# One more product of two identities on TensorE at each step of the first four edge passes

## The chip, the cores and the metric

One core of a Trainium2 chip. The time is the device time of one execution, in microseconds (us); of several executions the median is given.

## What is computed

A graph network of four layers over 3125 nodes of 256 features and 50,000 edges. The edges are sorted by destination. Every layer gathers a row per edge by its source, weights it, and sums the rows by destination; then come dense products, the residual and a layer norm.

```python
def _layernorm(x, axis=-1, eps=1e-05):
    m = jnp.mean(x, axis=axis, keepdims=True)
    v = jnp.var(x, axis=axis, keepdims=True)
    return (x - m) / jnp.sqrt(v + eps)

x = _layernorm(x + L0(x, src, dst, edge_weight))   # h=(1+eps)x+segment_sum(w*x[src],dst); relu(h@w1+b1)@w2+b2
x = _layernorm(x + L1(x, W, att, src, dst))        # 4 heads: softmax of leaky_relu(es[src]+ed[dst]) per dst, sum of alpha*z[src]
x = _layernorm(x + L2(x, ...))                     # two such attention layers (4 heads of 64, then 1 of 64), self loops added
x = _layernorm(x + L3(x, ...))                     # query-key attention, layer norm, FFN of 512, layer norm
```

Layer L2 has two passes over the edges, the others one each: five passes, called L0, L1, L2a, L2b and L3 in the code.

## The kernel before

The edges are cut into 416 steps (`STEPS`) of 128 edges, each within one block of 128 destination nodes. A pass runs over all steps. One step:

- GpSimd (POOL, L617) gathers the step's 128 source rows from a table in HBM by an indirect DMA into a slot of a ring (24 slots in L0, 48 in the others). It waits for `step_summed` of the step that had the slot before.
- The rows are scaled by their weight: in L0 by ScalarE (L1826, by the edge's weight), in L1 and L2a by VectorE (L1179), in L2b by VectorE (L1182), in L3 by ScalarE (L1887). This counts `row_scaled` up. In the last two groups of L1 and L2a (`HELPED`) ScalarE and GpSimd do a part of it.
- TensorE (PE) multiplies the step's one-hot matrix `M` (128 edges by 128 nodes of the block) with the rows into one of four PSUM banks (three in L3): L1551 in L0, L1655 in the others. It waits for the scaled rows, and for `sum_added` of the step that had the bank before. It counts `step_summed` up.
- VectorE adds the bank to the block's sums in `ACC` (L980 in L0, L1208 in the others, L1206 at a group's first step) and counts `sum_added` up.

All data is fp32, except where named. L0 also makes the one-hot matrices (VectorE, L966) and stores them to HBM; the later passes load them. Every 12 steps of L0 a small product on PE (L1541) transposes the destinations of 16 steps for VectorE (L905 to L915), which waits for it in the order of its own work.

The later passes work in groups of 16 steps (`GS`). For the softmax, a group's logits are picked (PE, L1607; in L3 `spread`, L1578, a product of 258 columns at each step, dotted with the rows by VectorE, L1084), transposed (L1616), scanned along the edges by VectorE (L1093 to L1164) with small products of PE between (L1623, L1628, L1635), exponentiated by ScalarE (L1850) and turned back (L1640). The sums run 32 steps behind the picks (`SOFAR` is 31). Each engine's order is written out in one loop over steps; on VectorE the addition of a step stands three positions behind the scaling, so that step k's rows are scaled right behind the addition of step k-4, which frees step k's bank.

Between the passes dense stages run (L1692, L1709, L1730). The change touches `sum_edges` (first pass) and `sum_step` in `gat_edges` (the other four), both on PE. `mm` is PE's matmul; `ident` is the 128 by 128 identity in fp32.

```python
for k in range(STEPS):                                                   # L0, PE
    pe.wait_ge(onehot_made.sem, onehot_made.at("L0", k + 1))
    pe.wait_ge(row_scaled.sem, row_scaled.at("L0", k + 1))
    if k >= 4:
        pe.wait_ge(sum_added.sem, sum_added.at("L0", k - 3))
    mm(PS[k % 4][:, 0:D], M[:, k % (4 * G), :], rows[:, k % RING["L0"], 0:D], start=True, stop=True)
```

## Time and profile before

| what | value |
|---|---|
| median of three runs | 3743.68 us (3743.38 to 3746.13) |
| the profiled execution | 3751.99 us |
| its span, first to last instruction | 3750.2 us |
| PE / PEld / DVE / ACT / POOL busy | 65% / 44% / 54% / 21% / 59% |
| mean granted clock of TensorE | 0.708 |
| DMA | 474.15 MB, 126 GB/s |

PE is TensorE's matmuls, PEld its weight loads, DVE VectorE, ACT ScalarE, POOL GpSimd. PEclk is the granted clock, as a share of full speed (2.4 GHz); it has two levels, 1 and 0.5. A fp32 product stands in the trace as two matmul instructions. Where the profile names "remote" or "another core or an unknown queue" as what ended a wait, it found no instruction that had ended shortly before the semaphore changed; this kernel has one core.

The first pass runs from 66 to 668 us, the others from 806, 1511, 2206 and 2985 us.

### The profile page before, as it was taken

The page shows a single profiled execution, that of the slowest core. Times are in us where ns is not written, and L with a number is a line of the kernel's source. Part 1 is how long each engine was busy: PE and PEld are TensorE (multiplying, and loading weights), DVE is VectorE, ACT ScalarE, POOL GpSimd, SP SyncE. Part 2 cuts the span into 40 slices and gives each one's busy share as a digit, 9 for nine tenths or more (in the row PEclk, how much of TensorE's full clock was granted, in tenths as well). Part 3 has the DMA queues.
Part 4 walks back from the last instruction along what each step waited for, and adds up shares of the span by engine and source line. Part 5 has one row for each costly group of instructions (what it writes and reads, how often), then busy time and mean ns, then how long its engine had stood idle before and what let it go on. Part 6 is the DMA issues. An engine that isn't in the chain of part 4 may idle for free.

```text
span 3750.2 us, 44316 instructions
## 1 busy us (share of the span) xinstructions
PE 2421.6 (65%) x9759; PEld 1656.7 (44%) x9759; DVE 2018.7 (54%) x7443; ACT 797.5 (21%) x2126; POOL 2225.6 (59%) x2434
## 2 busy tenths in 40 slices
PE   3564555936776774577677724444466688888887
PEld 1333333714444443344444514444453455555566
DVE  3554444626666674466666713333353366666677
ACT  1444445400000013000000300000002234443432
POOL 3666666466666646676666366666634366666535
PEclk8767666956666676566766755555555799999999
DMA  5665565145555543455555223333322255554411
GB/s 150 172 171 171 167 172 170 51 135 153 158 159 156 157 117 104 139 161 154 154 160 156 55 66 90 91 91 90 89 66 78 76 153 150 150 151 146 143 43 42
DMA packets 293515, 474.15 MB, mean 126 GB/s; under 512 B 63703, under 2 KB 166252, under 8 KB 293263
## 3 DMA queue, kind: packets, MB, share of 16 engines
q0 software_dynamic: 93184, 233.79, 23.9%
q1 hardware_dynamic: 200079, 237.52, 21.1%
q8 instruction: 95, 1.56, 0.2%
q14 instruction: 157, 1.29, 0.1%
HBM read 416.18 MB, written 54.91 MB: 126 GB/s over the span
## 4 chain that ended last, share of the span: by engine, by line
PE 45%; issue 21%; another core or an unknown queue 12%; DVE 11%; POOL 4%; ACT 2%; DMA 2%; DVEq 1%; SPq 0%; ACTq 0%; POOLq 0%
PE PS L1655 22%; PE PS L1578 5%; POOL work L617 4%; PE PS L1709 4%; PE PS L1551 4%; DVE ACC L1208 3%; PE PS L1730 2%; DVE work L1179 1%; PE PS L1692 1%; DMA work<-in_x,srcK 1%; PE PS L1635 1%; PE PS L1607 1%; PE PS L1764 1%; PE PS L1765 1%
## 5 line engine op out<-in xcount | busy, mean ns | idle before, releaser
L617 POOL DMA_INDIRECT work<-t_z,srcK x1248 | 1228.2, 984 | 635.4 <-issue 305.9
L1655 PE MATMUL PS<-work,M 128*128 128x260 f32 (+3 forms) x3328 | 1300.1, 511 | 469.2 <-issue 216.1
L1655 PEld LDWEIGHTS PS<-work,M 128*128 128x128 f32 x3328 | 750.6, 269 | 703.3 <-issue 494.6
L1208 DVE TENSOR_TENSOR ACC<-ACC,PS 128x260 f32 (+3 forms) x1614 | 589.3, 365 | 238.6 <-PE PS L1655 108.9
L617 POOL DMA_INDIRECT work<-t_x,srcK x416 | 395.7, 951 | 280.3 <-PE PS L1655 153.3
L617 POOL DMA_INDIRECT work<-in_x,srcK x416 | 397.3, 955 | 252.9 <-issue 116.0
L1551 PE MATMUL PS<-work,M 128*128 128x256 f32 x832 | 319.5, 525 | 269.0 <-issue 191.9
L1551 PEld LDWEIGHTS PS<-work,M 128*128 128x128 f32 x832 | 191.9, 256 | 390.8 <-issue 361.4
L1179 DVE TENSOR_TENSOR work<-work 128x256 f32<-128x256 f32 x800 | 328.2, 411 | 23.4 <-issue 19.9
L1841 ACT ACTIVATE work<-PS,group_begins 128x4 f32<-128x4 f32 (+1 forms) x100 | 26.2, 262 | 1446.7 <-remote 601.7
L1578 PE MATMUL PS<-Y,w 128*128 x832 | 284.4, 428 | 58.1 <-issue 37.4
L1607 PE MATMUL PS<-partsD,work 128*128 x1248 | 235.7, 198 | 115.3 <-DVE junk L1059 67.3
L980 DVE TENSOR_TENSOR ACC<-ACC,PS 128x256 f32 x416 | 173.4, 417 | 249.0 <-remote 141.0
L1607 PEld LDWEIGHTS PS<-partsD,work 128*128 128x128 bf16 x1248 | 181.3, 146 | 199.3 <-issue 144.8
L1826 ACT ACTIVATE work<-work,wK 128x256 f32<-128x256 f32 x416 | 195.9, 497 | 296.7 <-DMA work<-in_x,srcK 233.3
L1084 DVE SCALAR_TENSOR_TENSOR wz<-PS,work 128x258 f32<-128x258 f32 x416 | 173.0, 416 | 148.5 <-PE PS L1578 106.9
L522 POOL TENSOR_TENSOR rstd<-variance,minus_half 128x1 f32<-128x1 f32 x150 | 90.2, 611 | 225.6 <-DVE variance L1315 224.8
L1578 PEld LDWEIGHTS PS<-Y,w 128*128 128x128 f32 x832 | 147.1, 201 | 124.3 <-issue 106.9
L1887 ACT ACTIVATE work<-work 128x256 f32<-128x256 f32 x416 | 179.4, 494 | 0.1
L1149 DVE COPY work<-PS 64x2 f32<-64x2 f32 (+1 forms) x104 | 15.5, 149 | 229.3 <-remote 168.8
L966 DVE TENSOR_SCALAR M<-iota,dloc 128x128 f32<-128x128 f32 x416 | 121.5, 293 | 0.2
L1093 DVE TENSOR_TENSOR_SCAN work<-brk,PS 64x128 f32<-64x128 bf16 (+1 forms) x104 | 42.4, 408 | 145.0 <-remote 120.3
(240 smaller groups left out, 2816.6 us busy)
## 6 DMA issues: line engine op xcount, KB each, us to landing
M<-t_hot SPq DMA_DIRECT2D x416, 256.0 KB
work<-t_dhot SPq DMA_DIRECT2D x416, 128.0 KB
t_hot<-M SPq DMA_DIRECT2D x104, 256.0 KB
work<-t_z,srcK POOLq DMA_INDIRECT x1248
t_dhot<-work SPq DMA_DIRECT2D x104, 128.0 KB
work<-in_x,srcK POOLq DMA_INDIRECT x416
work<-t_edge SPq DMA_DIRECT2D x104, 64.0 KB
work<-t_x,srcK POOLq DMA_INDIRECT x416
```

The costliest lines, as they stand in the source:

```text
L617: pool.indirect_dma_start(out=slots[:, j, 0:width], out_offset=None, in_=table[:, :], in_offset=bass.IndirectOffsetOnAxis(ap=srcK[:, k:k + ...
L980: vec.tensor_tensor(a, a, PS[k % 4][:, 0:D], ALU.add).then_inc(sum_added.sem, 1)
L1084: vec.scalar_tensor_tensor(dots[:, k % 2, 0:ROWW], PS[3 + k % 2][:, 0:ROWW], float(D) ** -0.5, xring[:, k % RING["L3"], :], ALU.mult, ALU. ...
L1179: ins = vec.tensor_tensor(z, z, ring[:, j, width:width + heads].unsqueeze(2) .to_broadcast([P, heads, width // heads]), ALU.mult)
L1208: ins = vec.tensor_tensor(sums, sums, PS[k % SUMS[stage]][:, 0:cols], ALU.add)
L1551: mm(PS[k % 4][:, 0:D], M[:, k % (4 * G), :], rows[:, k % RING["L0"], 0:D], start=True, stop=True)\
L1578: mm(PS[3 + k % 2][:, 0:ROWW], dsthotF[c % 2][:, k % G * P:(k % G + 1) * P], at_block(Y, blocks[0][i])[:, 0:ROWW], start=True, stop=True). ...
L1607: mm(PS[4][:, at:at + 3 * heads], dsthot[:, c % 4, k % G * P:(k % G + 1) * P], at_block(partsD, blocks[0][i])[:, 0:3 * heads], start=True, ...
L1655: mm(PS[k % n][:, 0:cols], M[:, k % (4 * G), :], slots_of[:, k % RING[stage], 0:cols], start=True, stop=True)\
L1709: last = mm(bank[:, 0:cols], lhsT, rhs, start=k == 0, stop=k == len(left) - 1)
L1826: sc.activation(rows[:, j, 0:D], rows[:, j, 0:D], ACT.Copy, scale=wK[:, t:t + 1]).then_inc(row_scaled.sem, 1)
L1887: sc.activation(xring[:, j, 0:D], xring[:, j, 0:D], ACT.Copy, scale=xring[:, j, D:D + 1])\
```

## The change

At each step from the fifth on, PE now waits for the bank first, then multiplies the identity with the identity, broadcast twice (256 columns), into that bank, then waits for the step's rows and makes the sum into the same bank, which overwrites it. In the second to fourth pass this holds for steps 4 to 383, that is without the last two groups. In the fifth pass only the two waits change places. Nobody reads the added product and it signals nothing. The program gets it 1552 times: 412 and three times 380.

```diff
+            def keep_busy(bank):
+
+                mm(bank[:, 0:2 * P], ident[:], ident[:].unsqueeze(1).to_broadcast([P, 2, P]), start=True, stop=True)
+
             def sum_edges():
 
                 for k in range(STEPS):
+                    if k >= 4:
+                        pe.wait_ge(sum_added.sem, sum_added.at("L0", k - 3))
+                        keep_busy(PS[k % 4])
                     pe.wait_ge(onehot_made.sem, onehot_made.at("L0", k + 1))
                     pe.wait_ge(row_scaled.sem, row_scaled.at("L0", k + 1))
-                    if k >= 4:
-                        pe.wait_ge(sum_added.sem, sum_added.at("L0", k - 3))
                     mm(PS[k % 4][:, 0:D], M[:, k % (4 * G), :], rows[:, k % RING["L0"], 0:D], start=True, stop=True)\
                         .then_inc(step_summed.sem, 1)
...
                         pe.wait_ge(tops_put.sem, tops_put.at(stage, k // GS + 1))
-                    wait_scaled(pe, stage, k)
                     n = SUMS[stage]
                     if k >= n:
                         pe.wait_ge(sum_added.sem, sum_added.at(stage, k - n + 1))
+                        if stage != "L3" and k < STEPS - 2 * GS:
+                            keep_busy(PS[k % n])
+                    wait_scaled(pe, stage, k)
                     mm(PS[k % n][:, 0:cols], M[:, k % (4 * G), :], slots_of[:, k % RING[stage], 0:cols], start=True, stop=True)\
                         .then_inc(step_summed.sem, 1)
```

PE's order in the second pass, at a place where a group's small products stand, before (L1655 is the sum, L1607 the pick, L1628 and L1635 the small products):

```order
L1655 MATMUL PS<-work,M 128x260 [waits sum_added,row_scaled]
L1607 ISA [waits dsthot_moved2]
L1607 MATMUL PS<-partsD,work 128x12
L1655 MATMUL PS<-work,M 128x260 [waits sum_added,row_scaled]
L1628 MATMUL PS<-ones,work 64x1 [waits fan_made]
L1628 MATMUL PS<-ones,work 64x1
L1635 MATMUL PS<-work,ones 128x4 [waits alphas_put,climb_taken]
```

And with the change (L1662 is the sum, L1546 the added product, L1612 the pick, L1633 and L1640 the small products):

```order
L1546 MATMUL PS<-ident 128x256 [waits sum_added]
L1662 MATMUL PS<-work,M 128x260 [waits row_scaled]
L1612 ISA [waits dsthot_moved2]
L1612 MATMUL PS<-partsD,work 128x12
L1546 MATMUL PS<-ident 128x256 [waits sum_added]
L1662 MATMUL PS<-work,M 128x260 [waits row_scaled]
L1633 MATMUL PS<-ones,work 64x1 [waits fan_made]
L1633 MATMUL PS<-ones,work 64x1
L1640 MATMUL PS<-work,ones 128x4 [waits alphas_put,climb_taken]
```

In front of each sum there is now a product that takes over its wait for the bank; the small products stand behind one more of them each.

PE's order in the first pass, around the transposing product L1541, before (12 sums between two of them):

```order
L1541 MATMUL PS<-ident,work 64x128 [waits breaks_made,tables_v]
L1551 MATMUL PS<-work,M 128x256 [waits sum_added,row_scaled,onehot_made] x12
L1541 MATMUL PS<-ident,work 64x128 [waits breaks_made,tables_v]
```

And with the change, from the last sums ahead of one such product to the first behind it (L1556 is the sum):

```order
L1546 MATMUL PS<-ident 128x256 [waits sum_added]
L1556 MATMUL PS<-work,M 128x256 [waits row_scaled,onehot_made]
L1541 MATMUL PS<-ident,work 64x128 [waits breaks_made,tables_v]
L1546 MATMUL PS<-ident 128x256 [waits sum_added]
L1556 MATMUL PS<-work,M 128x256 [waits row_scaled,onehot_made]
```

The transposing product keeps its place; 12 sums between two of them have become 12 pairs.

## Rows read from the trace of the kernel before

**Rows 1.** The page: busy time by engine, the clock in 40 slices, the chain by engine
```profile
PE 2421.6 (65%) x9759; PEld 1656.7 (44%) x9759; DVE 2018.7 (54%) x7443; ACT 797.5 (21%) x2126; POOL 2225.6 (59%) x2434
...
PEclk8767666956666676566766755555555799999999
...
PE 45%; issue 21%; another core or an unknown queue 12%; DVE 11%; POOL 4%; ACT 2%; DMA 2%; DVEq 1%; SPq 0%; ACTq 0%; POOLq 0%
```

**Rows 2.** Stretches of the five passes: length, busy time of PE, PEld, DVE, ACT, POOL (instructions), clock, DMA
```profile
66.00:668.00 602.00, 340.72 (x948) 204.19 (x948) 290.54 (x1009) 293.06 (x620) 384.88 (x404) 0.70 0.60 171
806.00:1425.00 619.00, 439.73 (x1562) 271.45 (x1563) 399.08 (x1342) 38.16 (x138) 391.94 (x403) 0.67 0.52 145
1511.00:2123.00 612.00, 437.31 (x1601) 272.44 (x1602) 393.98 (x1297) 36.18 (x148) 392.44 (x392) 0.67 0.52 146
2206.00:2818.00 612.00, 317.32 (x1587) 262.00 (x1587) 237.35 (x1266) 24.82 (x92) 360.88 (x392) 0.50 0.35 85
2985.00:3588.00 603.00, 503.58 (x2101) 349.79 (x2099) 375.66 (x1537) 248.50 (x608) 350.05 (x368) 0.94 0.49 144
```

**Rows 3.** Timeline of POOL, 352 to 358 us: start, length, what, idle before and releaser
```profile
352.36 0.94 POOL L617 DMA_INDIRECT work<-in_x,srcK  x1 [0.30 <-issue]
356.02 0.95 POOL L617 DMA_INDIRECT work<-in_x,srcK  x1 [2.72 <-PE PS L1551]
357.27 0.95 POOL L617 DMA_INDIRECT work<-in_x,srcK  x1 [0.30 <-issue]
```

**Rows 4.** Chains by line, in 500 us of each of the five passes, in their order
```profile
by line: issue 24.6%; PE PS L1551 22.1%; POOL work L617 21.9%; another core or an unknown queue 10.9%; DMA work<-in_x,srcK 8.8%; DVE ACC L980 3.5%; ACT work L1826 2.2%; ACT work L1812 1.4%; DVE M L966 1.0%; PE PS L1541 0.7%; DVE brk L864 0.
by line: PE PS L1655 40.5%; issue 17.8%; another core or an unknown queue 14.3%; DVE ACC L1208 7.7%; DVE work L1179 4.8%; PE PS L1635 1.7%; PE PS L1607 1.5%; PE PS L1628 1.4%; DVEq L340 1.1%; DVE junk L1059 1.1%; PE PS L1640 1.0%; DVEq L120
by line: PE PS L1655 36.2%; issue 31.1%; another core or an unknown queue 10.1%; DVE ACC L1208 5.8%; DVE work L1179 3.4%; PE PS L1635 1.8%; PE PS L1607 1.5%; PE PS L1628 1.5%; PE PS L1640 0.9%; DVEq L340 0.8%; DVE junk L1059 0.7%; DVE work 
by line: issue 37.5%; PE PS L1655 36.4%; another core or an unknown queue 12.1%; PE PS L1607 2.7%; DVE ACC L1208 2.5%; PE PS L1635 2.4%; DVE work L1182 2.2%; PE PS L1623 1.1%; PE PS L1616 0.8%; PE PS L1628 0.8%; DVEq L1208 0.6%; PE PS L1640
by line: PE PS L1578 33.7%; PE PS L1655 27.2%; issue 14.7%; another core or an unknown queue 4.3%; PE PS L1593 3.9%; PE PS L1594 2.8%; ACT work L1887 2.2%; DVE wz L1084 1.9%; PE PS L1635 1.5%; ACT w L1882 1.2%; DVE ACC L1208 1.0%; PE PS L15
```

**Rows 5.** Timeline of a stall in the first pass, PE, then DVE
```profile
345.87 0.43 PE L1541 MATMUL PS<-ident,work 128*64 128x128 f32 x2
346.23 1.13 PE L1551 MATMUL PS<-work,M 128*128 128x256 f32 x4
352.66 0.77 PE L1551 MATMUL PS<-work,M 128*128 128x256 f32 x1 [5.30 <-issue]
...
345.55 0.30 DVE L966 TENSOR_SCALAR M<-iota,dloc 128x128 f32<-128x128 f32 x1
351.55 0.28 DVE L905 COPY work<-PS 64x128 f32<-64x128 f32 x1 [5.71 <-remote]
...
355.89 0.42 DVE L980 TENSOR_TENSOR ACC<-ACC,PS 128x256 f32 x1 [2.33 <-PE PS L1551]
```

**Rows 6.** Groups of PE's L1709; then the stretch 340.6 to 344.4 us of L1551 alone
```profile
L1709 PE MATMUL PS<-wff,work 128*128 128x256 f32 x200 | 47.1, 379 | 0.0
...
340.60:344.40 3.80, 3.80 (x9) 2.95 (x10) 0.50 0.56 178
```

**Rows 7.** Waits of 850 to 1350, then of 100 to 600 us: total, times, longest
```profile
PE PS L1655 <- DVE work L1179: 58.2, 22, 7.2
PEld PS L1655 <- DVE work L1179: 56.4, 39, 7.5
...
PE PS L1551 <- DVE ACC L980: 34.8, 21, 4.3
PE PS L1551 <- ACT work L1826: 13.1, 6, 3.9
```

**Rows 8.** Two stretches of the first pass, columns as in rows 2
```profile
345.00:352.00 7.00, 2.36 (x11) 1.35 (x9) 0.92 (x3) 3.43 (x8) 5.48 (x6) 0.98 0.70 201
352.00:362.00 10.00, 7.58 (x17) 5.22 (x18) 6.45 (x24) 5.08 (x11) 5.74 (x7) 0.50 0.53 159
```

## The prediction

> **What bounds the kernel now.** I read the page first, for the clock and the chain, then the stretches of the five passes, then the chain and the waits inside them, then one stall in order of time.
>
> TensorE ran at 0.708 of full speed on the mean, and the clock row is low up to the fourth pass and high behind it [rows 1]. The passes over the edges are 602, 619, 612, 612 and 603 us long, with granted clocks of 0.70, 0.67, 0.67, 0.50 and 0.94 and PE busy for 57%, 71%, 71%, 52% and 84% of them [rows 2]. So the fifth pass, which makes a product of 258 columns more at each step (the query's spread), is the one at full clock. The change gives the first four passes a product of much that size too. It does not touch what lies outside them.
>
> Is PE what these passes wait for? GpSimd's gathers are not the bound: when nothing holds them back they start 1.25 us apart (0.95 busy, 0.30 idle), so 416 of them want 520 us, 82 to 99 us less than a pass takes, and the gather at 356.02 started when a sum on PE had made its ring slot free, after 2.72 us of idling [rows 3]. A pass is a loop of PE's sum, VectorE's addition of it and the scaling of rows further on. In the chains of the passes PE's sum has 22.1%, 40.5%, 36.2% and 36.4% (L1551, L1655) [rows 4].
>
> The chain also has waits put to "another core or an unknown queue". There is one core; rows of one stall show what these are. The transposing product at L1541 was issued at 345.87 and took 0.43 us by the trace, but VectorE, whose L905 waits for it, started at 351.55 after 5.71 us of idling with the releaser given as "remote"; the sum issued behind it at 346.23 was added only at 355.89 [rows 5]. PE's results thus reach others several us late at times, and VectorE stands still meanwhile. Such waits have 10.9%, 14.3%, 10.1% and 12.1% of the chains of the first four passes, and 4.3% of the fifth's [rows 4]. The pass with the busiest PE and the highest clock has the fewest. That is the observation on which my forecast rests; that the load is the cause is a guess, since the fifth pass differs in more.
>
> **The change, part by part.** Counts: 412 added products in the first pass (steps 4 to 415), 380 in each of the next three (steps 4 to 383), 1552 in all. Each is two matmul instructions of 256 columns with their weight loads. Nothing is moved on VectorE and SyncE, and on the others only line numbers change.
>
> *Price of one product.* At full clock, 200 such instructions back to back were busy for 47.1 us: 0.24 us each, 0.47 a product. At half clock, 9 of them filled 3.80 us: 0.42 each, 0.84 a product [rows 6].
>
> *What the clock gives back.* Work that takes B at clock c takes B c/0.94 at the fifth pass's clock. PE's busy time per pass would go from 340.7 to 254, from 439.7 to 313, from 437.3 to 312 and from 317.3 to 169 us [rows 2]. With 412 x 0.47 = 194 and 380 x 0.47 = 179 us added: 448, 492, 491 and 348 us, or 74%, 79%, 80% and 57% of the passes. So even with the clock held PE is busy for 107, 52, 54 and 31 us more than now. Only what lies on the chain counts; by the share of the sum there (22.1%, 40.5%, 36.2%, 36.4%) that is 24 + 21 + 20 + 11 = **76 us lost**.
>
> *What hides it.* The product stands in front of the wait for the row, so it is free where PE stands there. In 500 us of the second pass 61 waits of PE and its weight loads on the scaled row (L1179) came to 115 us [rows 7]; one product fits into each, so at most 61 x 0.47 = 29 us, of the 158 us that the products of that stretch take (416 steps x 500/619 = 336, by 0.47). In the first pass the waits are for the bank instead (L980, 34.8 us, against 13.1 for the row, L1826) [rows 7], and the added product stands behind that wait: nothing is hidden. I count nothing for this.
>
> *The moved wait.* The bank's wait now comes ahead of the row's. Both must be met before the sum in any case, so in the fifth pass, which has no added product, I cost it at 0. In the others PE's later picks and turns stand behind the added product, and whoever waits for them (VectorE's scans, ScalarE's exponentials) waits up to 0.47 us longer; that is in the 76 us.
>
> *Late results.* Bounds: no gain, and the whole of these waits (11.8% of 2445 us, 289 us). With PE's load at 74%, 79% and 80% the first three passes come near the fifth's 84%, so I take its share of 4.3% for them: 6.6% of 602, 10.0% of 619 and 5.8% of 612 us are 40 + 62 + 35 us. The fourth stays at 57%, so half of its 7.8%: 24 us. Together **161 us won**.
>
> *Sum.* The profiled execution took 3751.99 us; 3752 + 76 - 161 = 3667. The median of the runs, 3743.68, is 8.3 us lower, so about **3659 us**.
>
> A rule weighed against this: the order of work on PE. In rows 5 the sum issued behind the late product was added later still, so one late or long product holds what is behind it. The Trainium skill, page "PSUM — Partial Sum Buffer", section "Engine vs sequencer instructions", says that matmuls start and complete in program order. By that rule a product that nobody reads delays every sum behind it by its own length wherever PE is not waiting; this is the mechanism of rival (a). With it the sum has the 76 us lost, without it (the added product standing aside) it would have none and end at 3583.
>
> And on the clock: in 345 to 352 us the clock was at its higher level (2.4 GHz) and PE stood still for 5.3 us; in 352 to 362 us it was at the lower (1.2 GHz) [rows 5, 8]. The Trainium skill, page "TensorE: Matmul & The Clock Gate", section "What's actually happening", says that the throttled state is the default and activity releases it. It speaks for the change only if the added products fill the gaps; here the gap is a wait for the bank, ahead of the product.
>
> **Rivals.**
> (a) *The added product only stands in the way; slower.* The late results stay as they are, because they come after PE has run out of work at the bank's wait, where the product can't run. Place: the sum loop of the passes. Price with the clock held: +76 us, 3752 + 76 = 3828, in the runs' terms 3820. It decides once late results shrink by less than 76 of 289 us. If the clock is held only in part it is worse: with clocks as now (40%, 34%, 34% and 0% of the time at full speed) a product costs 0.69, 0.71, 0.71 and 0.84 us and nothing comes back, 412 x 0.69 x 0.221 + 380 x (0.71 x 0.767 + 0.84 x 0.364) = 63 + 323 = 386 us; half way between is +231, 3975. For it: stalls of 5 us before the product [rows 5], little hiding [rows 7]. Against it: the fifth pass, with the same load, is at 0.94 and no longer than the others.
> (b) *Both cancel; no change.* The fifth pass takes 603 us with its extra product, the first 602 without one [rows 2]: that the load costs what the clock brings is what this row says if read alone. Time 3744.
> (c) *The late results go altogether.* 3752 + 76 - 289 = 3539, 3531 in the runs' terms; the gathers' floor (365 us below now) isn't reached. For it: nothing but the trend of rows 4.
>
> **Chances.** Forecast 0.42, (a) 0.38, (b) 0.12, (c) 0.08. Something like 0.2%, 7.5 us, is what a measurement of this kernel can tell from no change; (b) spreads about evenly over such a band and both sides of it. Faster by more: 0.42 + 0.08 and a little of (b), 0.52; within: 0.08; slower: 0.40. The range leaves out (c), and the part of (a) in which the clock is not held: from 3590, where late results go for three quarters (3744 + 76 - 217 is 3603, less something for hiding), to 3880, which takes (a)'s 3820 and a fifth of the way from there to its worst end, the 386 us. The likeliest case alone spans 3600 to 3720.
>
> **What would show it.** Right: granted clock of 0.9 or more in the first three passes and clearly over 0.5 in the fourth; PE busy near 448, 492, 491 and 348 us; "another core" near 4% in the chains of the first three; the sum's steps 1.39 to 1.44 us apart where they are 1.45 to 1.49 now (pass by 416). Wrong in favour of (a): VectorE's waits on L905, L1093, L1117 and L1149 with the releaser "remote" as long as before, and the sum with the added product over half of the chain. If the clock in the first pass is below 0.8, the term "what the clock gives back" is the one that failed. The fifth pass should be as long as before.

## The result and the profile after

The changed kernel took **3779.93 us** (median of 4 runs, 3774.89 to 3788.83), the kernel before 3744.9 us on the same chip (4 runs, 3743.38 to 3750.77). The ratio is 1.0094, interval 1.0081 to 1.0107: **35 us slower**, where 3659 us was forecast. The profiled execution took 3774.89 us.

The page of the changed kernel (busy time, clock, chain by engine, the added product's group), to be laid beside [rows 1]:

```profile
PE 2830.4 (75%) x12863; PEld 2112.1 (56%) x12863; DVE 2020.4 (54%) x7443; ACT 797.0 (21%) x2126; POOL 2219.3 (59%) x2434
...
PEclk8988888969999996799999857777675789999999
...
PE 58%; issue 16%; DVE 9%; another core or an unknown queue 8%; POOL 3%; ACT 2%; DMA 2%; DVEq 1%; SPq 0%; ACTq 0%; POOLq 0%
...
L1546 PE MATMUL PS<-ident 128*128 128x256 f32 x3104 | 1196.7, 472 | 304.9 <-issue 223.2
```

The five passes, columns as in [rows 2]:

```profile
64.00:681.00 617.00, 470.17 (x1771) 359.94 (x1772) 291.58 (x1011) 292.77 (x620) 384.10 (x405) 0.87 0.60 168
818.00:1443.00 625.00, 502.46 (x2327) 355.35 (x2328) 399.81 (x1343) 38.80 (x141) 392.14 (x404) 0.91 0.51 144
1528.00:2144.00 616.00, 492.99 (x2362) 350.21 (x2362) 395.48 (x1296) 36.42 (x149) 390.13 (x392) 0.93 0.51 145
2226.00:2847.00 621.00, 487.14 (x2348) 405.29 (x2348) 237.13 (x1268) 24.79 (x92) 360.53 (x392) 0.71 0.34 84
3013.00:3611.00 598.00, 497.79 (x2104) 346.81 (x2102) 375.87 (x1537) 249.12 (x609) 348.80 (x368) 0.95 0.49 146
```

The chains by line in 500 us of the first and of the fourth pass, to be laid beside the first and fourth of [rows 4]:

```profile
by line: PE PS L1546 24.0%; PE PS L1556 22.6%; issue 16.6%; POOL work L617 11.7%; DMA work<-in_x,srcK 8.1%; another core or an unknown queue 7.9%; DVE ACC L980 2.7%; ACT work L1833 2.0%; ACT work L1819 1.1%; PE PS L1541 0.9%; ACT work L1825
```

```profile
by line: PE PS L1546 46.1%; issue 18.0%; PE PS L1662 15.6%; another core or an unknown queue 8.9%; DVE ACC L1208 1.7%; PE PS L1612 1.7%; DVE work L1182 1.5%; PE PS L1640 1.4%; PE PS L1645 1.0%; PE PS L1628 0.8%; PE PS L1633 0.6%; PE PS L164
```

The clock came up as meant: 0.87, 0.91, 0.93 and 0.71 where it was 0.70, 0.67, 0.67 and 0.50. Yet each of the four passes is longer, by 15, 6, 4 and 9 us, 34 us together; the fifth is 5 us shorter, and so is by 6 us what lies outside the passes. (The two profiled executions differ by 23 us, the medians by 35.) In the first pass the sum and the added product now fill 46.6% of the chain, where the sum had 22.1% [rows 4]; "another core" went from 10.9% to 7.9%.

Did the late results go? VectorE's longest waits, of the kernel before and then of the changed one (what waits, for whom, total us, times, longest):

```profile
DVE work L1149 <- remote: 168.8, 38, 13.6
DVE ACC L980 <- remote: 141.0, 36, 11.2
DVE work L1093 <- remote: 120.3, 32, 6.5
DVE ACC L1208 <- PE PS L1655: 108.9, 95, 2.6
...
DVE ACC L1208 <- remote: 106.8, 40, 3.8
...
DVE ACC L980 <- PE PS L1551: 42.5, 33, 3.2
```

```profile
DVE ACC L1208 <- PE PS L1662: 264.8, 170, 3.9
DVE work L1149 <- remote: 150.3, 45, 13.3
DVE ACC L980 <- PE PS L1556: 128.4, 85, 4.4
...
DVE ACC L980 <- remote: 97.6, 25, 13.6
DVE work L1093 <- remote: 83.0, 31, 3.8
...
DVE ACC L1208 <- remote: 25.0, 16, 2.7
```

The waits with the releaser "remote" shrank on the two additions (141.0 to 97.6, 106.8 to 25.0 us), and those put to PE's sum grew by more (42.5 to 128.4, 108.9 to 264.8). All of VectorE's idle time before the two additions, of the kernel before and then of the changed one (the last numbers are busy us, mean ns, idle us and what ended most of it):

```profile
L1208 DVE TENSOR_TENSOR ACC<-ACC,PS 128x260 f32 (+3 forms) x1614 | 589.3, 365 | 238.6 <-PE PS L1655 108.9
...
L980 DVE TENSOR_TENSOR ACC<-ACC,PS 128x256 f32 x416 | 173.4, 417 | 249.0 <-remote 141.0
```

```profile
L1208 DVE TENSOR_TENSOR ACC<-ACC,PS 128x260 f32 (+3 forms) x1614 | 589.6, 365 | 327.6 <-PE PS L1662 264.8
...
L980 DVE TENSOR_TENSOR ACC<-ACC,PS 128x256 f32 x416 | 173.4, 417 | 263.0 <-PE PS L1556 128.4
```

Over the whole kernel VectorE's "remote" waits fell from 828 to 566 us, and yet it waits longer for the sums than before. A wait that loses this name isn't a wait that is gone.

A fact for the reading of all that follows: the kernel before ran at two speeds on the chips of this study, with medians of 3712 to 3745 us in the first jobs and 3231 to 3235 us in the later ones, without a run in between. One chip had both, 3712.5 us in an early job and 3231.5 us in a later one. Each experiment is compared with runs of the kernel before beside it; what makes the difference is a main result below, and what sets it on was not found.

### The profile page after: what moved, and what is told of

The parts are those of the page before. It is cut to its first block, busy times and chain, and to the rows that moved or that the text cites. A ratio compares the mean times of both kernels' runs of the same rounds, so it can differ in the third digit from the quotient of the medians.

```text
span 3773.1 us, 49623 instructions
## 1 busy us (share of the span) xinstructions
PE 2830.4 (75%) x12863; PEld 2112.1 (56%) x12863; DVE 2020.4 (54%) x7443; ACT 797.0 (21%) x2126; POOL 2219.3 (59%) x2434
## 4 chain that ended last, share of the span: by engine, by line
PE 58%; issue 16%; DVE 9%; another core or an unknown queue 8%; POOL 3%; ACT 2%; DMA 2%; DVEq 1%; SPq 0%; ACTq 0%; POOLq 0%
PE PS L1546 19%; PE PS L1662 15%; PE PS L1583 6%; PE PS L1716 4%; PE PS L1556 4%; POOL work L617 3%; DVE ACC L1208 3%; PE PS L1737 2%; DMA work<-in_x,srcK 1%; PE PS L1699 1%; PE PS L1612 1%; PE PS L1640 1%; DVE work L1179 1%; PE PS L1771 1%
## 5 line engine op out<-in xcount | busy, mean ns | idle before, releaser
L1546 PE MATMUL PS<-ident 128*128 128x256 f32 x3104 | 1196.7, 472 | 304.9 <-issue 223.2
L1662 PE MATMUL PS<-work,M 128*128 128x260 f32 (+3 forms) x3328 | 995.9, 388 | 110.6 <-issue 65.9
L1662 PEld LDWEIGHTS PS<-work,M 128*128 128x128 f32 x3328 | 700.0, 218 | 287.8 <-issue 133.4
L1546 PEld LDWEIGHTS PS<-ident 128*128 128x128 f32 x3104 | 576.7, 221 | 471.6 <-issue 350.7
L1208 DVE TENSOR_TENSOR ACC<-ACC,PS 128x260 f32 (+3 forms) x1614 | 589.6, 365 | 327.6 <-PE PS L1662 264.8
L1179 DVE TENSOR_TENSOR work<-work 128x256 f32<-128x256 f32 x800 | 329.3, 412 | 23.9 <-issue 19.5
L980 DVE TENSOR_TENSOR ACC<-ACC,PS 128x256 f32 x416 | 173.4, 417 | 263.0 <-PE PS L1556 128.4
L1556 PE MATMUL PS<-work,M 128*128 128x256 f32 x832 | 279.5, 422 | 8.2 <-DVE M L966 8.2
L1612 PE MATMUL PS<-partsD,work 128*128 x1248 | 213.0, 181 | 82.0 <-DVE junk L1059 62.6
L1612 PEld LDWEIGHTS PS<-partsD,work 128*128 128x128 bf16 x1248 | 152.2, 123 | 135.9 <-issue 102.0
L1556 PEld LDWEIGHTS PS<-work,M 128*128 128x128 f32 x832 | 180.5, 217 | 40.5 <-issue 8.5
L1149 DVE COPY work<-PS 64x2 f32<-64x2 f32 (+1 forms) x104 | 15.5, 149 | 210.0 <-remote 150.3
```

What stands on the lines that cost most here:

```text
L980: vec.tensor_tensor(a, a, PS[k % 4][:, 0:D], ALU.add).then_inc(sum_added.sem, 1)
L1179: ins = vec.tensor_tensor(z, z, ring[:, j, width:width + heads].unsqueeze(2) .to_broadcast([P, heads, width // heads]), ALU.mult)
L1208: ins = vec.tensor_tensor(sums, sums, PS[k % SUMS[stage]][:, 0:cols], ALU.add)
L1546: mm(bank[:, 0:2 * P], ident[:], ident[:].unsqueeze(1).to_broadcast([P, 2, P]), start=True, stop=True)
L1612: mm(PS[4][:, at:at + 3 * heads], dsthot[:, c % 4, k % G * P:(k % G + 1) * P], at_block(partsD, blocks[0][i])[:, 0:3 * heads], start=True, ...
L1662: mm(PS[k % n][:, 0:cols], M[:, k % (4 * G), :], slots_of[:, k % RING[stage], 0:cols], start=True, stop=True)\
```

## The experiments

### Parts of the change

**e1_waits_only**: the two waits change places, no product.

```diff
                     if k >= 4:
                         pe.wait_ge(sum_added.sem, sum_added.at("L0", k - 3))
-                        keep_busy(PS[k % 4])
...
-                        if stage != "L3" and k < STEPS - 2 * GS:
+                        if False:
```

> The change without the added products: only the wait for the bank stands ahead of the wait for the row, in all five passes. Theory T1 (the added product itself costs TensorE time that lies on the path): same as before, within 4 us of 3744, fifth pass 603 us. Rival T2 (the moved wait delays TensorE, since two waits one after the other are met later than both at once): 10 to 35 us slower than before.

3710.06 us against 3712.48, ratio 0.9993 (0.998 to 1.0005). The moved wait costs nothing.

**e2_first, e3_second_third, e4_fourth**: the products in the first pass alone (412), in the second and third (760), in the fourth (380). The edit is the same condition, narrowed (this is e4's; e2 makes it false for the later passes, e3 and e4 also take the product out of the first pass):

```diff
-                        if stage != "L3" and k < STEPS - 2 * GS:
+                        if stage == "L2b" and k < STEPS - 2 * GS:
```

> Added products in the first pass alone (412). T1: all passes pay by their own, so +12 to +18 us (the first pass was 617 us instead of 602 with the change), the other passes as before. T3 (the loss comes from the fourth pass, where the clock was held least, 0.71, and PE's busy time rose most): first pass within 5 us of before.

> Added products in the second and third pass alone (760). T1: +5 to +12 us (625 and 616 us with the change, 619 and 612 before), clock 0.91 and 0.93 there. T3: no loss or a gain of some us, since PE waits least for the bank there and the clock is held.

> Added products in the fourth pass alone (380). T1: about +9 us (621 us with the change, 612 before) and clock 0.71 there. T3: +25 to +35 us, nearly the whole loss of the change.

Against 3712.48 us: 3727.26 (ratio 1.0039, 1.0022 to 1.0056), 3726.53 (1.0034, 1.002 to 1.0047) and 3721.84 (1.0022, 1.0009 to 1.0036), or +15, +14 and +9 us. They add up to 38 us, near the change's 35. Every pass pays for its own products, 0.02 to 0.04 us for each, of the 0.77 us that one is busy (1196.7 by 1552).

### The size of the product

**e5_bf16, e6_64cols, e7_twice**: the identities read as bf16, so that a product is one matmul instruction of 256 columns; 64 columns in fp32; the whole product twice.

```diff
-                mm(bank[:, 0:2 * P], ident[:], ident[:].unsqueeze(1).to_broadcast([P, 2, P]), start=True, stop=True)
+                half = ident[:].bitcast(mybir.dt.bfloat16)
+                mm(bank[:, 0:2 * P], half[:, 0:P], half[:, 0:2 * P], start=True, stop=True)
```

```diff
-                mm(bank[:, 0:2 * P], ident[:], ident[:].unsqueeze(1).to_broadcast([P, 2, P]), start=True, stop=True)
+                mm(bank[:, 0:64], ident[:], ident[:, 0:64], start=True, stop=True)
```

```diff
                 mm(bank[:, 0:2 * P], ident[:], ident[:].unsqueeze(1).to_broadcast([P, 2, P]), start=True, stop=True)
+                mm(bank[:, 0:2 * P], ident[:], ident[:].unsqueeze(1).to_broadcast([P, 2, P]), start=True, stop=True)
```

> The change with the identities read as bf16 (half columns of the fp32 tile), still 256 columns: one matmul instruction instead of two, about a quarter of the length. T1 (what is lost is PE's time on the path, what is won is the clock): if the clock is held as with the fp32 product, over 0.85 in the first three passes, 40 to 80 us faster than before; if the clock stays near 0.7, 5 to 10 us slower. T4 (the clock is worth nothing here, because the passes are paced by the turns between the engines): the clock may rise, the time stays within 10 us of before.

> The added product with 64 columns instead of 256, fp32 as before, two weight loads and two matmuls. T1: between before and the change by a quarter of the length: PE's added busy time a half or less, clock between 0.71 and 0.85; -20 to +15 us. T4: +5 to +15 us, by its length and its weight loads alone.

> The added product made twice at each step. The clock can hardly rise further in the second and third pass (0.91, 0.93). T1: each product more is 0.43 to 0.47 us on PE with nothing given back: the loss is far more than double, 1552 x 0.45 = 700 us of PE time, a third to two thirds of it on the path, +230 to +470 us against before. T4 (turns between the engines pace it, PE has room): +35 to +90 us.

Against 3712.46 us: bf16 3722.61 (1.0025, 1.0013 to 1.0037; mean clock 0.739), 64 columns 3758.77 (1.0125, 1.0105 to 1.0145; clock 0.73), twice 3809.28 (1.0268, 1.0251 to 1.0285; clock 0.923). The price doesn't follow the clock: 64 columns left it at 0.73 and cost 46 us, more than 256 columns, and twice the products put it at 0.98, 0.97, 0.98 and 0.91 in the four passes and cost more than anything else. That e6 costs so much was expected by no theory. The first four passes of e6, columns as in [rows 2], tell more:

```profile
64.00:673.00 609.00, 441.36 (x1772) 335.87 (x1772) 290.32 (x1010) 292.78 (x620) 383.40 (x404) 0.76 0.61 170
812.00:1436.00 624.00, 519.16 (x2327) 374.52 (x2328) 402.31 (x1343) 38.58 (x141) 390.00 (x404) 0.72 0.51 144
1521.00:2133.00 612.00, 532.57 (x2362) 386.60 (x2362) 396.30 (x1295) 36.31 (x149) 383.59 (x392) 0.70 0.52 146
2216.00:2833.00 617.00, 473.27 (x2348) 424.99 (x2349) 237.09 (x1265) 24.98 (x93) 360.64 (x392) 0.50 0.35 84
```

PE is busy for 1966 us in them, a little longer than with 256 columns (1953 us in the four passes of the changed kernel). Each of e6's matmul instructions is shorter, 368 ns on the mean against 472, but at the lower clock the sums take longer. Set beside PE's busy time in the four passes, the prices under this condition follow it:

| products | PE busy in the four passes, us | cost, us |
|---|---|---|
| none (e1, e8, the kernel before) | 1509 to 1536 | 0 |
| bf16 (e5) | 1565 | 10 |
| every other step (e12, below) | 1774 | 23 |
| the change; behind the waits (e11, below) | 1953; 1929 | 35; 42 |
| 64 columns (e6) | 1966 | 46 |
| twice (e7) | 2351 | 97 |

From e12 on that is some 0.1 us for each us that PE is busy longer. It is an order, not a mechanism: why a tenth of it shows isn't shown.

### Where the product stands, and how many there are

**e11_behind_waits** puts the product behind all of the step's waits; **e12_every_other** makes it at odd steps only.

```diff
                     if k >= 4:
                         pe.wait_ge(sum_added.sem, sum_added.at("L0", k - 3))
-                        keep_busy(PS[k % 4])
                     pe.wait_ge(onehot_made.sem, onehot_made.at("L0", k + 1))
                     pe.wait_ge(row_scaled.sem, row_scaled.at("L0", k + 1))
+                    if k >= 4:
+                        keep_busy(PS[k % 4])
... (the same in the later passes)
```

```diff
-                        if stage != "L3" and k < STEPS - 2 * GS:
+                        if stage != "L3" and k < STEPS - 2 * GS and k % 2:
... (the same in the first pass)
```

> The changed kernel with each product behind all of the step's waits, directly in front of the step's sum, so that no wait can take it up. T1 (TensorE's time is on the path; the place in front of the wait covers a part of it): it costs much more than the change, by 0.45 us of each product whose step waited for its row (17 to 50 per cent of 1552: 120 to 350 us more). T4 (a step has room of its own, and what shows of a product is a small share wherever it stands): within 30 us of the changed kernel, at 1.006 to 1.018 of the kernel before.

> The changed kernel with a product at every second step of the same passes (some 776 of 1552). T4: half the products, half the cost, +10 to +25 us over the kernel before, and a TensorE clock between the two. By the late results alone (the price is a fixed one for a pass that holds products): as much as the change, +30 to +40. If it is no slower than the kernel before or faster, the higher clock gave back what the products took.

Against 3741.5 us: 3783.74 (1.0112, 1.0092 to 1.0132) and 3764.35 (1.006, 1.0043 to 1.0078). Behind the waits it costs 42 us, as in front of them within the intervals: the place in front of the wait for the row hides nothing that can be measured. Half the products cost 23 us (16 to 29 by the interval), between half of the change's price and the whole; a fixed price for a pass that holds products, 30 to 40 us whatever their number, doesn't fit.

**e8_later_wait** leaves the product out and lets VectorE come for the first pass's transposing product (L1541) three steps later, so that a late result of it would be covered.

```diff
-                elif q == 5:
+                elif q == 8:
```

> No added product: the kernel before, where VectorE in the first pass waits for the transposing product L1541 three steps later (positions 8 to 11 of 12 instead of 5 to 8). If late results of PE hold up the first pass, it loses most of the 46 us in 500 that VectorE waited for this one and gets 20 to 50 us shorter. If they only stand beside another bound (the gathers, or the clock), the first pass stays within 5 us of 602 and the wait moves to another line.

3713.2 us, ratio 1.0003 (0.9994 to 1.0013); its first pass took 594 us, as e1's did (595). VectorE's wait for L1541 was gone, and its waits before the addition of the sum (L980) grew from 232 to 298 us in that pass (e1 against e8). To cover this one late result wins nothing.

### The gathers

If neither PE's time nor one late result sets the pace, what does? **e9_plain_rows** and **e10_plain_rows_product** take the indirect DMAs out of the kernel before and of the changed one. Plain copies of 128 consecutive rows stand in their place, so these kernels sum other rows than the graph's.

```diff
-                    pool.indirect_dma_start(
-                        out=slots[:, j, 0:width], out_offset=None, in_=table[:, :],
-                        in_offset=bass.IndirectOffsetOnAxis(ap=srcK[:, k:k + 1], axis=0)).then_inc(landing(stage, k).sem, 16)
+                    pool.dma_start(out=slots[:, j, 0:width], in_=table[(k % 24) * P:(k % 24 + 1) * P, 0:width])\
+                        .then_inc(landing(stage, k).sem, 16)
```

> The kernel before, in which each step's 128 rows come by one plain copy from 128 consecutive rows of the same table (in turn from 24 places), on GpSimd's queue, where they were gathered by index: it computes with other rows than the graph's, everything else is left. T5 (the gathers of GpSimd's queue set the pace of the passes, and what is seen on TensorE is their echo): the passes fall from some 595 to 615 us to under 560 us each, the whole to under 3500 us. T4 (the turns between TensorE, VectorE and ScalarE set the pace): the five passes stay within 10 us of what they are, the whole within 50 us of 3712 us.

> The changed kernel with the same plain copies in place of the gathers (other rows than the graph's). Against the kernel before with plain copies: by T4, and by T1 the more, the products cost at least the 35 us that they cost with gathers. By T5, where the gathers had paced the passes and covered the most of the products, they cost clearly more than 35 us once these are gone, up to the 0.3 to 0.45 us of each of 1552 products, 470 to 700 us. If the products instead cost nothing here, the 35 us came from how product and gather meet.

Beside 3741.5 us for the kernel before, e9 took 2552.97 (ratio 0.6819, 0.679 to 0.6847) and e10 2692.13 (0.7192, 0.718 to 0.7204). The passes of e9, same columns; the first was 602 us long and the fourth 612 [rows 2]:

```profile
64.00:404.00 340.00, 286.75 (x948) 144.94 (x948) 284.28 (x1009) 284.98 (x615) 211.79 (x392) 0.96 0.92 302
514.00:954.00 440.00, 360.17 (x1563) 220.33 (x1564) 388.98 (x1340) 38.36 (x140) 223.02 (x407) 0.85 0.68 208
...
1481.00:1815.00 334.00, 303.90 (x1587) 262.75 (x1587) 233.34 (x1263) 24.83 (x92) 210.79 (x401) 0.50 0.56 158
```

The same sums, additions and turns fit into 340, 440 and 334 us; the fourth pass at a clock of 0.50. No wait in e9 has the releaser "remote". So the gathers set the pace, and the late results go with them. Once they are gone, PE's time shows: the products cost 139 us.

How can gathers do that, when they want 520 us of 602? The trace has an entry whenever a semaphore is incremented. I laid these entries beside the gathers' queue in the kernel before. Three of the longer pauses of that queue, all for want of a free slot, and what came in them:

```
end of the last gather        pause           first burst of increments
300.95                        300.95-303.57   302.54 to 302.58, 5 increments; 303.31 and 303.36, sums
335.84                        335.84-338.53   338.26 to 338.43, 17 increments, 4 of them of the sums
353.31                        353.31-356.02   355.72 to 356.02, 12 increments, 4 of them of the sums
```

While gathers follow each other at 1.25 us, increments come late, those of DMAs as well as PE's (in the bursts above all others are of DMAs, but for one of the transposing product); PE, VectorE and ScalarE stand; the gathers run on until the ring is full; some 2.4 us after the last one, in these three, the held increments arrive in a bunch; the engines catch up and it begins again.

Counted from the 61st gather of each pass on. A pause is over 0.5 us between two gathers; a bunch is three or more increments of the sum, three within 0.35 us; "beyond 0.30" is the pauses' time without the usual 0.30 us each:

```
                    first     second    third     fourth pass
before  bunches     25        20        16        43      each begins in a pause
        pauses      45        42        42        56
        beyond 0.30 69        59        56        77 us
after   bunches     38        28        28        42      each begins in a pause
        pauses      62        58        53        68
        beyond 0.30 78        66        61        84 us
```

A sum's increment also ends such a pause, since it frees the slot, so that bunches and pauses would fall together in any case. Two more counts speak for the pause coming first. None of the 240 bunches begins within 0.9 us of the end of the last gather (0.92 to 2.50 us after it). And the entries of all semaphores, DMAs' included, stay few while gathers are issued, 3.0 to 4.7 per us in the four passes of the kernel before, and in the first us of a pause (1.7 to 3.5); after that us they come at 7.5 to 14.6 per us. In the kernel of e17 below, without late increments, they come at 22 to 26 per us under the same train of gathers. In e9 78 plain copies followed each other without a pause (1464 to 1505 us), with 45 entries per us.

A pass is 416 gathers at 1.25 us, 520 us, with the pauses and the ends: 520 + 69 and some 13 for the first pass's 602; 40, 36 and 15 us for the ends of the next three, where e17, without pauses, has 41, 34 and 20 beyond 520. The added product doesn't move the 520. With it the pauses are more, though each is shorter (1.56 us on the mean in the first pass, 1.83 before), and their time grows by 9 + 7 + 5 + 7 = 28 us, of the 34 by which the passes grew (in the first pass 9 of 15).

Two experiments were to tell the gathers' time on their queue from their effect on others; both came to run where the kernel before takes 3231.5 us.

**e13_plain_slowed, e14_plain_slowed_product**: plain copies, each followed by a memset.

```diff
+                    if spared[0]:
+                        pool.wait_ge(spare_set.sem, spared[0])
+                    spared[0] += 1
+                    nc.gpsimd.memset(spare[:], 0.0).then_inc(spare_set.sem, 1)
... (the copy in place of the gather as in e9; `spare` and its semaphore are declared above)
```

> The kernel before with plain copies in place of the gathers (other rows than the graph's), and behind each copy a memset of 128x448 of a spare tile on GpSimd, so that its queue takes about 1.2 us a step, near the 1.25 us of a gather. T5a (the gathers set the pace by their time on the queue alone): the passes come back to 590 to 620 us, the whole to 3650 to 3750 us, and TensorE's results come late again or are seen not to matter. T5b (the gathers set the pace by making TensorE's results late): the passes take 416 times the queue's new pace and some 15 us, near 520 us each at 1.2 us, the whole 3200 to 3350 us, and no wait of VectorE has a releaser that the profile can't name.

> The changed kernel with the same slowed plain copies. T5b: with GpSimd's queue as the pace and no late results the products lie in the slack of each step and cost within 10 us of e13. If they cost 35 us or more here too, it isn't the late results but TensorE's own chain with VectorE that shows them.

2728.76 us and 2792.1 us, ratios 0.8443 (0.8424 to 0.8462) and 0.8645 (0.8631 to 0.8659). The memset took 0.49 us and ran beside the copy's issue in part, so that the queue's pace became 0.94 us a step, not 1.2. The first and fourth passes followed it (400 and 422 us, 416 by 0.94 is 391), and there the products cost 6 and 3 us; the second and third took 453 and 432 us and paid 22 and 35 us. The expected 10 us in all for e14 failed, 63 were measured: in e14 PE is busy for 450 of 475 us in the second pass and 447 of 467 in the third, so at 0.94 us a step the passes with the wide sums have no slack left. At that pace, and where nothing is late in the kernel before either, e13 can't tell the gathers' time on the queue from their effect on others.

**e15_narrow_gathers**: in the first pass gathers of 64 of the 256 numbers.

```diff
+                part = width if stage != "L0" else width // 4
+                quarter = table.rearrange("r (a b) -> (r a) b", b=part)
...
-                        out=slots[:, j, 0:width], out_offset=None, in_=table[:, :],
+                        out=slots[:, j, 0:part], out_offset=None, in_=quarter,
```

> The kernel before with gathers of a quarter row (64 of 256 numbers) in the first pass alone: as many gathers, as many rows of each, other numbers than the graph's; GpSimd zeroes the slots once before them. If the bytes in flight make TensorE's results late, the first pass falls from 602 us towards 520 to 560 us; if it is the number of gathers or of their rows, it stays within 10 us, and the late results stay with it.

3235.69 us, ratio 1.002 (1.0007 to 1.0033). Since no result was late on this chip, it can't answer what it was made for. It shows only that the bytes don't set the gathers' pace: 1.25 us apart, as with whole rows, and a first pass of 517 us, as in e17.

### The kernels again, where increments come in time

**e16_after_again**, **e17_before_again** and **e18_twice_again** are the changed kernel, the kernel before and e7's kernel without a further edit.

> The changed kernel again, beside the kernel before, to see it where the kernel before takes 3231 us, if it comes to such a chip. Where the gathers' queue sets the pace (3231 us) and no results come late: the products lie in the slack of the first and fourth passes (at most 5 us each, as in e13 and e14: 400 to 406 and 422 to 425 us) and cost 5 to 15 us each in the second and third, where the sums are wider, so +10 to +40 us in all. Where the kernel before takes 3710 to 3745 us: +30 to +40 us, as before.

> The kernel before, unchanged, for its profile where it takes 3232 us (if it comes to such a chip). By T5b: GpSimd's gathers are 1.25 us apart with no time in which a full ring holds them, the five passes take 490 to 560 us, the part of the chain that has no releaser in the profile is 0 to 1 per cent of the span, where it was 12 per cent at 3744 us, and the durations of TensorE's and VectorE's instructions at one clock are what they were.

> The changed kernel with each product made twice, again. Where the kernel before takes 3232 us and the gathers' queue sets the pace at 1.25 us a step: two products of 0.43 us at the high clock beside 0.5 to 0.8 us of other work of TensorE fill the step, so the first and fourth passes grow by under 15 us each, the second and third by 30 to 70 us each, in all +60 to +150 us. Where the kernel before takes 3710 us or more: +97 us, as before.

e16: 3236.8 us against 3231.73, ratio 1.0016 (1.0005 to 1.0027). That is less than the 10 to 40 us expected. e17: 3239.03 us (one execution; the others on that chip 3230 to 3239). e18: 3437.65 us against 3235.04, ratio 1.0624 (1.0606 to 1.0642). The kernel before in e17, its chain on the page and its passes:

```profile
PE 46%; DMA 15%; POOL 13%; issue 11%; DVE 9%; DVEq 3%; ACT 2%; SPq 1%; POOLq 0%; ACTq 0%
```

```profile
64.00:581.00 517.00, 338.62 (x948) 197.36 (x948) 296.51 (x1010) 291.09 (x618) 386.34 (x405) 0.80 0.67 198
698.00:1259.00 561.00, 383.49 (x1565) 237.85 (x1566) 394.19 (x1341) 38.52 (x140) 412.51 (x421) 0.75 0.58 165
1320.00:1874.00 554.00, 380.13 (x1602) 237.58 (x1602) 390.57 (x1298) 36.50 (x149) 405.05 (x412) 0.77 0.59 166
1932.00:2472.00 540.00, 306.87 (x1588) 263.69 (x1588) 238.13 (x1264) 24.80 (x92) 379.60 (x411) 0.50 0.40 98
2584.00:3075.00 491.00, 462.17 (x2104) 331.75 (x2103) 371.73 (x1539) 249.67 (x609) 351.61 (x370) 1.00 0.60 178
```

What GpSimd's gathers wait for, in the kernel before at 3750 us of span, then in e17:

```profile
POOL work L617 <- issue: 513.9, 1612, 3.3
POOL work L617 <- PE PS L1655: 287.9, 275, 53.0
POOL work L617 <- remote: 254.2, 148, 5.2
```

```profile
POOL work L617 <- issue: 446.0, 1463, 0.3
...
POOL work L617 <- PE PS L1655: 145.7, 478, 0.3
```

"Another core" is gone from the chain, and no gather within a pass waits over its usual 0.3 us: the passes run at the gathers' 1.25 us, 517 to 561 us. The passes are 385 us shorter together (3048 to 2663 us by the stretches), the work outside them 128 us: 513 us of span in all. The number of increments that the trace holds tells the conditions apart at a glance: 21,946 before against 68,738 in e17, and 69,442 in e9, which ran beside 3741.5 us but without gathers. Where they are late, two of three have no entry of their own (of the DMAs' 12,601 are left of 54,231, of the sums' 1,527 of 2,061). A wait whose increment has no entry goes under "issue"; "remote" is a wait whose increment has an entry long after the instruction that made it had ended. So both names grow by the same fault, and neither gives its size. VectorE's own instructions took what they take in the kernel before (L980 416 and 417 ns on the mean, L1179 409 and 411).

The changed kernel under this condition (first, second and fourth pass), then twice the products in the same three:

```profile
64.00:582.00 518.00, 436.12 (x1772) 325.01 (x1772) 296.86 (x1012) 292.65 (x620) 385.55 (x405) 0.95 0.68 199
699.00:1259.00 560.00, 474.88 (x2326) 354.76 (x2326) 399.15 (x1340) 38.67 (x140) 410.06 (x420) 0.92 0.59 165
...
1937.00:2477.00 540.00, 436.73 (x2349) 372.29 (x2349) 244.52 (x1268) 24.91 (x93) 379.16 (x411) 0.74 0.41 98
```

```profile
65.00:631.00 566.00, 564.23 (x2596) 479.23 (x2596) 297.39 (x1011) 293.00 (x620) 383.52 (x405) 1.00 0.65 182
748.00:1379.00 631.00, 608.76 (x3084) 484.62 (x3084) 406.25 (x1340) 38.55 (x140) 403.62 (x421) 0.97 0.53 147
2127.00:2669.00 542.00, 512.49 (x3108) 447.61 (x3108) 244.42 (x1268) 24.84 (x92) 380.00 (x412) 0.94 0.40 98
```

Three of the four passes keep their length to a microsecond with one product a step (the third grows by 5 us); one product lies whole in the slack under the gathers, though the clock goes from 0.80, 0.75 and 0.50 to 0.95, 0.92 and 0.74. Two products fill PE in the first and second pass (564 of 566 and 609 of 631 us), and these become PE's; the fourth, with 512 of 542, stays the gathers'. I had expected +60 to +150 us for e18 and saw +203, since the first pass grew by 49 us, not under 15, and the second and third by 70 and 76. It is the second floor of these passes: e7, with late increments, took 635 us for its second pass and e18, without, 631.

None of the kernels that compute the reference's result is faster than the kernel before. The runs point to the gathers. Fewer and larger gathers, or a queue that pauses on purpose before the ring is full, weren't tried.

## Why the prediction was wrong

**"GpSimd's gathers are not the bound."** This failed first. The arithmetic was right, 520 us of 602, and so was the row: a gather that had waited 2.72 us for a slot [rows 3]. What it meant was read the wrong way round. The ring wasn't full because a sum took long; the gathers had run on while the increments hung, and these came 0.9 us or more after the last gather. e9 shows who sets the pace: without gathers 340 us for the 602, with as many instructions of PE. e17 shows the floor at work: 517.

**Late results, 161 us won.** The term that turned the sign: the four passes were to win 161 us against 76 lost, and they grew by 34. The stall of [rows 5] is real, but a busier PE doesn't do away with it: e7 kept PE busy for 586 of 628 us in the first pass and made it longer. The fifth pass, the model for the gain, has few "remote" waits of VectorE (67 us, where the first has 188), and still it goes from 603 to 491 us in e17: few waits of that name didn't mean little loss. The share of "another core" fell from 10.9, 14.3, 10.1 and 12.1% to 7.9, 9.6, 4.8 and 8.9% with the change, and VectorE's waits turned up under PE's name. The size was off too: what late increments cost in all is 512 us (3744 against 3232), not 289, which is more than their share in any chain, since they also hold PE, and waits without an entry stand under "issue" (21% of the chain, 11% in e17).

**Price of a product, 0.47 us, and what the clock gives back.** Right in the first three passes: PE was busy for 470, 502 and 493 us where 448, 492 and 491 were forecast. At full clock a second product adds 0.42 us (e18's first pass less e10's, 564.2 and 390.1 us, by 412). The fourth pass's clock, taken as 0.94, was 0.71: PE was busy for 487 us there, 139 more than forecast.

**76 us lost.** Forecast 24, 41 and 11 us for the first, the second with the third, and the fourth pass; e2 to e4 measured 15, 14 and 9. The total was twice too large, and the way to it wrong: a share of a chain isn't a price. With the busy times that PE came to, the same shares give 29 + 25 + 20 + 62 = 136 us. And L1655 has 22% of the page's chain in the kernel before and 21% in e17, so that the product should cost about the same under both conditions; it cost 35 and 5 us.

**Nothing hidden by the row's wait; the moved wait free; the fifth pass unchanged.** Right: e11 (42 against 35 us, intervals overlapping), e1 (0.9993), 603 to 598 us. The 61 waits on the scaled row were counted too high: a weight load and the sum behind it stand still for the same row, and [rows 7] has both. As nothing was counted for them, this changed no term.

**Order of work on PE.** The Trainium skill, page "PSUM — Partial Sum Buffer", section "Engine vs sequencer instructions", says that matmuls start and complete in program order. e18 is in keeping with it: once PE is full (564 of 566 us), the passes are as long as its products take. Where PE has slack, as in e16, the product delays nothing that counts (518 us, where e17 has 517).

**Rivals.** (a) named the outcome, with a price of 76 us where 35 came. It decided by "late results shrink by less than 76 us". By name they shrank by more: VectorE's waits on L905, L1093, L1117 and L1149 with the releaser "remote" went from 422 to 341 us, those on the two additions by 125. In effect they didn't, as the passes show. The sum with the added product has 46.6%, 49.7%, 58.6% and 61.7% of the chains, over half in two of the four. (c) took the late results' end for 3531; the e17 condition went to 3232. The steps were 1.48 us apart in the first pass (617 by 416), not 1.39 to 1.44.

## What to carry to other kernels

A wait put to an unknown core, in a program on one core, was here an increment that came long after its instruction had ended: count the increments in the trace, and look what every engine and queue does when they come in bunches, before pricing the wait. A full ring doesn't show that the consumer is slow: take the producer's transfers away once (plain copies in place of gathers, wrong rows) and see what the rest can do; that run would have settled this case first. And a higher clock for an engine is worth only what its time is worth: here 0.71 to 0.85 for the whole kernel brought nothing under either condition.

## What the runs showed of the hardware

- With gathers at 1.25 us a step, increments of PE's and of the DMAs' semaphores came late, and in bunches in the pauses of the gathers' queue (1.6 to 1.8 us on the mean in the kernel before; never sooner than 0.9 us after the last gather). With plain copies from the same queue, at 0.81 us a step in the first pass of e9, they didn't. Under the other condition neither did, at the same 1.25 us. What differs between the two conditions of the chips, and what in a gather does it, stays open: it isn't one chip's property (one had both), and e15, which cut the bytes, ran where nothing was late. Nor do the runs tell whether the recording of the trace has a part in it: none is known to be without a record. The Trainium skill, page "DMA: Bandwidth & Descriptors", section "SWDGE vs HWDGE vs iDMA", says that GpSimd computes these DMAs' descriptors itself, plain and indirect alike; no run here shows whether that has to do with it.
- The same program took 3744 and 3232 us, a difference of 14% and fifteen times the effect under study.
- Of PE's clock: 1552 products of 256 columns in fp32 brought the mean from 0.708 to 0.852, the same number in bf16 0.739, 64 columns in fp32 0.73, twice the fp32 ones 0.923.
